# A graph network's gathers through a ring of eight lots instead of four

## The reference

```
h = relu(layernorm(x));  x = x + layer(h)          # four times

layer 0:  msg = relu(h[src] + edge_attr);           agg = segment_sum(msg, dst)
          out = ((1 + eps) * h + agg) @ W.T + b
layer 1:  relational attention: messages of 86 edge types from 16 bases,
          weighted by tanh(relu(score)), summed over dst, and a self loop
          that takes the source of each node's last edge
layer 2:  msg = edge_weight * h[src];               agg = segment_sum(msg, dst)
          out = relu(agg @ W + b)
layer 3:  msg = h[src];                             agg = segment_sum(msg, dst)
          out = agg @ W.T + b
```

## Time and profile before

| | us |
|---|---|
| median of 3 runs | 10165.41 |
| the profiled execution | 10155.89 |
| its span, first to last instruction | 10154.0 |
| POOL busy | 6668.1 (66%) |
| PE busy | 4395.6 (43%) |
| DVE busy | 4403.6 (43%) |
| ACT busy | 2227.0 (22%) |
| mean granted clock of TensorE | 0.538 |

### The profile page before, as it was taken

How to read it: one execution, slowest core, us unless ns; L and a number is a source line. 1 busy time by engine, 2 the same in 40 slices (tenths; PEclk the granted TensorE clock), 3 DMA queues, 4 the chain that set the end, 5 groups by cost and what they waited for, 6 DMA issues and landing times.

```text
span 10154.0 us, 102607 instructions
## 1 busy us (share of the span) xinstructions
PE 4395.6 (43%) x23835; PEld 3937.0 (39%) x23836; DVE 4403.6 (43%) x8860; ACT 2227.0 (22%) x5821; POOL 6668.1 (66%) x6577
## 2 busy tenths in 40 slices
PE   4444444444466666666663232222233232332223
PEld 3333333333366666666662222222222222222222
DVE  5444444444377777777773222222222222222222
ACT  0000000000477777777770000000000000000000
POOL 5666666664477777777775666666665666666665
PEclk6555555555655555555555555555555555555555
DMA  3111111111477777777771000000000000000001
GB/s 69 22 22 22 22 22 22 22 22 31 160 219 221 219 219 219 218 219 218 220 217 26 11 11 11 11 11 11 11 11 16 11 11 11 11 11 11 11 11 16
DMA packets 601171, 726.23 MB, mean 72 GB/s; under 512 B 341132, under 2 KB 434892, under 8 KB 597969
## 3 DMA queue, kind: packets, MB, share of 16 engines
q0 software_dynamic: 290064, 544.60, 21.8%
q1 hardware_dynamic: 311081, 181.32, 6.5%
HBM read 685.46 MB, written 40.38 MB: 71 GB/s over the span
## 4 chain that ended last, share of the span: by engine, by line
another core or an unknown queue 35%; issue 24%; POOL 22%; DVE 10%; DMA 3%; ACT 2%; PE 1%; DVEq 1%; POOLq 0%; SPq 0%; ACTq 0%
POOL arena L502 13%; POOL lanes L502 9%; DVE arena L978 3%; DMA lanes<-table,idx 2%; DVE arena L950 2%; DVE arena L942 1%; DVE lanes L942 1%; DVE lastrow L973 1%; ACT arena L699 1%; DMA arena<-table,idx 1%; DVE ps L937 0%; DVE lanes L968 0%; DVE lanes L1086 0%; ACT arena L685 0%
## 5 line engine op out<-in xcount | busy, mean ns | idle before, releaser
L502 POOL DMA_INDIRECT lanes<-table,idx x4764 | 4501.0, 945 | 2652.7 <-issue 1435.1
L1214 PE MATMUL ps<-arena,lanes 128*128 128x128 f32 x9528 | 2429.8, 425 | 4543.4 <-DVE arena L950 1844.0
L1214 PEld LDWEIGHTS ps<-arena,lanes 128*128 128x128 f32 x9528 | 2072.7, 303 | 4878.1 <-issue 4798.9
L502 POOL DMA_INDIRECT arena<-table,idx x1664 | 2049.1, 1231 | 676.9 <-issue 507.0
L551 ACT COPY idx<-tabs 128x4 int32 (+1 forms) x1616 | 303.0, 194 | 6851.8 <-DMA lanes<-table,idx 6698.3
L937 DVE TENSOR_TENSOR ps<-ps,tabs 128x16 f32<-128x16 f32 x1191 | 211.4, 177 | 3458.9 <-remote 3121.0
L1214 PE MATMUL ps<-lanes 128*128 128x32 f32 x3328 | 791.6, 402 | 666.0 <-issue 414.3
L1214 PEld LDWEIGHTS ps<-lanes 128*128 128x128 f32 x3328 | 750.3, 330 | 693.1 <-issue 693.0
L950 DVE TENSOR_TENSOR arena<-lanes,ps 128x512 f32<-128x512 f32 x794 | 543.7, 685 | 985.2 <-DMA lanes<-table,idx 944.6
L1311 PE MATMUL ps<-t,arena 128*128 x3328 | 955.5, 402 | 0.0
L1311 PEld LDWEIGHTS ps<-t,arena 128*128 128x128 f32 x3328 | 859.8, 318 | 0.0
(11 more groups left out here) (201 smaller groups left out, 3028.7 us busy)
## 6 DMA issues: line engine op xcount, KB each, us to landing
arena<-step_rows SPq DMA_DIRECT2D x416, 256.0 KB
lanes<-table,idx POOLq DMA_INDIRECT x4764
arena<-table,idx POOLq DMA_INDIRECT x1664
table<-arena SPq DMA_DIRECT2D x24, 1088.0 KB, 4.9
lanes<-in_edge_attr SPq DMA_DIRECT2D x388, 64.0 KB
table<-h SPq DMA_DIRECT2D x18, 256.0 KB, 2.4
edge_rows<-arena SPq DMA_DIRECT2D x1, 2496.0 KB, 8.4
lanes<-self_loop_table,selfi POOLq DMA_INDIRECT x98
```

Of the source, the lines that this page charges most:

```text
L502: pool.indirect_dma_start(out=to[:, k, u, :], out_offset=None, in_=tableD[l], in_offset=bass.IndirectOffsetOnAxis(ap=idx[:, k, u:u + 1], a ...
L1214: last = mm(ps[:, bass.ds(w[u], rhs.shape[-1])], onehot[:, k, u, :], rhs, start=False, stop=True, skip_group_check=True)
```

## The change

The ring of the wide layers becomes eight lots (`RING = 8`, `ROUND` = 32 tiles), so rows, attributes, indices, masks, both one-hot matrices and messages have eight slots. Only the sum with the attributes (`total`) keeps four. The narrow layer keeps its ring of four with arrays of its own (`idx1`, `onehot`, `msg`). In the wide layers each signal of an engine becomes one semaphore that counts lots through all three layers: `wide_idx_ready`, `total_ready`, `masked`, `weighted`, `wide_msg_ready` and `wide_mm_done`. A wait names the number of lots that must be done. What DMAs signal stays one semaphore for each slot, now eight. Layer 2 has 49 full rounds and five more lots, as have 0 and 3; no unused slots are counted up any more.

```diff
 LOTS, HB = 4, 4
 BODY = LOTS * HB
-STEPS_W = -(-(TILES + EXW) // BODY) * BODY
+RING = 8
+ROUND = RING * HB
+STEPS_W = -(-(TILES + EXW) // ROUND) * ROUND
+WIDE_LOTS = -(-(TILES + EXW) // HB)
+ROUNDS, REST = WIDE_LOTS // RING, WIDE_LOTS % RING
+BEFORE = {0: 0, 2: WIDE_LOTS, 3: 2 * WIDE_LOTS}
...
-        idx = sb("idx", [P, LOTS, HB], I32)
+        idx = sb("idx", [P, RING, HB], I32)
+        idx1 = sb("idx1", [P, LOTS, HB], I32)
...
-        masked = lotwise("mask_ready")
-        weighted = lotwise("weighted_mask_ready")
+        wide_idx_ready = sem("wide_idx_ready")
+        wide_gathered = [sem(f"wide_gathered_{h}") for h in range(RING)]
+        attr_loaded = [sem(f"attr_loaded_{h}") for h in range(RING)]
+        total_ready = sem("total_ready")
+        masked = sem("mask_ready")
+        weighted = sem("weighted_mask_ready")
+        wide_msg_ready = sem("wide_msg_ready")
+        wide_mm_done = sem("wide_scatter_done")
...
             with sp.Fori(0, MAIN) as i:
-                for k in range(LOTS):
-                    sp.wait_ge(row_used[k], i + 1)
+                for k in range(RING):
+                    sp.wait_ge(total_ready, i * RING + (k + 1))
...
+                def wide(i, lots):
+
+                    for k in range(lots):
+                        n = pool.to_reg(i * RING + (BEFORE[l] + k + 1))
+                        pool.wait_ge(written[0], written[1])
+                        pool.wait_ge(wide_idx_ready, n)
+
+                        pool.wait_ge(total_ready if l == 0 else wide_msg_ready, n)
+                        for u in range(HB):
+                            gather(grow[:, k, u, :], idx[:, k, u:u + 1], wide_gathered[k])
...
             def lots(l):
+
+                with act.Fori(0, ROUNDS - 1) as i:
+                    for k in range(RING):
+                        gathered_by(l, i, k)
+                        wide_lot(i + 1, k)
...
+                if l != 3:
+                    for k in range(RING):
+                        wide_lot(0, k)
...
+            def lots_to(l, i, k):
+
+                return i * RING + (BEFORE[l] + k + 1)
+
             def masks(l, i, k):
 
-                dve.wait_ge(mm_done[k], i + (BEFORE[l] + 1))
+                dve.wait_ge(wide_mm_done, lots_to(l, i, k))
                 tt(mask[:, k], iota_ps[:, 0:WB].unsqueeze(1).to_broadcast([P, HB, WB]), per_edge(BLK, i, k), ALU.is_equal
-                   ).then_inc(masked[k], 1)
+                   ).then_inc(masked, 1)
...
-                    tt(total[:, k], grow[:, k], attr[:, k], ALU.add).then_inc(row_used[k], 1)
-                    onehots(i, k, onehot)
+                    tt(total[:, k % LOTS], grow[:, k], attr[:, k], ALU.add).then_inc(total_ready, 1)
+                    onehots(i, k, onehotw)
...
+            def scatter(l, i, k, w):
+
+                pe.wait_ge(wide_msg_ready, i * RING + (BEFORE[l] + k + 1 + RING))
                 for u in range(HB):
...
-                last.then_inc(mm_done[k], 1)
+                last.then_inc(wide_mm_done, 1)
...
+                def body(i, lots):
+                    for k in range(lots):
+                        if k % LOTS == 0:
+                            w = windows(i * ROUND + k * HB, min(BODY, (lots - k) * HB))
+                        scatter(l, i, k, w[k % LOTS * HB:])
```

More of the change, by code:

```diff
@@ L52 @@
 XW = EXN + TILES
[L53 to L57, removed]
+NARROW = STEPS_N // BODY
+WIDE_LOTS = -(-(TILES + EXW) // HB)
+ROUNDS, REST = WIDE_LOTS // RING, WIDE_LOTS % RING
+BEFORE = {0: 0, 2: WIDE_LOTS, 3: 2 * WIDE_LOTS}
+TURN = {0: 0, 2: 1, 3: 2}
+MAIN = (N_EDGES // P) // ROUND
+TAIL = STEPS_W - MAIN * ROUND
+assert 0 < REST and MAIN + 1 == ROUNDS
 P1_LOTS = -(-BLOCKS // 4)
@@ L492, in _, with gather, narrow @@
                         pool.wait_ge(*written)
[L494 to L496 removed]
+                def gather(into, index, there):
+                    pool.indirect_dma_start(
+                        out=into, out_offset=None, in_=tableD[l],
+                        in_offset=bass.IndirectOffsetOnAxis(ap=index, axis=0)).then_inc(there, 16)
+                def narrow(n):
+                    for k in range(LOTS):
                         pool.wait_ge(written[0], written[1])
                         pool.wait_ge(idx_ready[k], n)
[L500 removed]
+                        pool.wait_ge(row_used[k], n)
                         for u in range(HB):
[L502 to L510, removed]
+                            gather(g1[:, k, u, :], idx1[:, k, u:u + 1], gathered1[k])
+                def wide(i, lots):
[6 more added lines that the diff above has]
+                            gather(grow[:, k, u, :], idx[:, k, u:u + 1], wide_gathered[k])
+                if l == 1:
+                    with pool.Fori(1, NARROW + 1) as n:
+                        narrow(n)
+                else:
+                    with pool.Fori(0, ROUNDS) as i:
+                        wide(i, RING)
+                    wide(ROUNDS, REST)
         @block.scalar
@@ L586, in linear @@
                 if l:
-                    for k in range(LOTS):
-                        act.wait_ge(mm_done[k], BEFORE[l + 1] + 1)
+                    act.wait_ge(wide_mm_done, BEFORE[l] + WIDE_LOTS + RING)
                     sums(0)
@@ L995, in scattered @@
             def scattered(l):
-                for k in range(LOTS):
-                    dve.wait_ge(mm_done[k], BEFORE[l + 1] + 1)
+                if l == 1:
+                    for k in range(LOTS):
+                        dve.wait_ge(mm_done[k], NARROW + 1)
+                else:
+                    dve.wait_ge(wide_mm_done, BEFORE[l] + WIDE_LOTS + RING)
             scattered(0)
```

186 lines of the change are left out of this document (96 added, 90 removed).

## The result

The changed kernel takes 10069.53 us (median of 4 runs, 10062.59 to 10080.74) and the kernel before 10168.27 (4 runs, 10157.7 to 10177.35): a ratio of 0.9904, 95% interval 0.9887 to 0.9921. It is 98.7 us faster. The forecast was 9850, so the direction is right, and the gain is less than a third of the 313 us forecast; the time lies outside the forecast's own range of 9760 to 10065, inside the wide one.

The account below looks back on a forecast made before the run. POOL's stops in layers 0, 2 and 3, from PE's signals held back while POOL gathers without pause. Savings 88 + 142 + 83 = 313 us off 10155.9, plus 9.5 for the median: 9850; own range 9760 to 10065, wide 9350 to 10160.

Parts of the forecast that it names:

- What bounds the kernel now: No engine is full; POOL's waits for DVE in layers 0, 2 and 3 total 1117.6 us, a deeper ring's most.
- PE is not late; its signal is: Layer 2: matmuls that DVE waits for had ended 37 and 24 us before DVE learned of it.
- the signals of x1 to x3 come in time for x5 to x7: Layer 2, lots numbered from DVE's release: signals of the first three scatters arrive in time for the lots four places on.
- 13 lots a cycle: Layer 2 with eight slots: POOL stops every 13 lots where it was 8, giving 30.5 stops.
- The stop was 8.05; I take 8.3: Layer 2: each POOL stop takes 8.3 us, 253 us in all, 142 less than 395.3.
- Layer 0: POOL stops every 8 lots for 6.0 us, the middle of two cases: 298 us in all, 88 less.
- Counters at nothing: Counting semaphores cost nothing; upper end 357 us, for a whole POOL pause of 0.30 us per lot.
- At a layer's end ... all at nothing, with some 5 us either way: ACT copies eight indices instead of four beside a layer's last scatters; this and other small changes cost nothing, 5 us either way.
- A: Signals are at most some 40 us late, so POOL never stops: 9047, or about 9600 with half the stops; chance 0.14.
- C: POOL issues four gathers between short pauses, such a lot costing 8.8 us instead of 5.9: 10520; chance 0.11.
- B: POOL's stops grow with its runs, so the ring buys nothing: 10165, between 10120 and 10185; chance 0.18.
- The rule of the Trainium skill: The block taking profile records holds up its producers rather than lose one inside; if so, records count, not the ring: 10165.

Follow-up runs that it names:

- the kernel with a gather in 1.55 us: Changed kernel with a POOL memset of 128x192 after each gather of the wide layers; 10450.38 us, 1.0423 of the kernel before.
- the short pause: Changed kernel with a POOL memset of 128x32 after each gather of the wide layers; 10089.44 us, 0.9898 of the kernel before.

## Why the prediction was wrong in size

**What bounds the kernel now.** Right in the main. POOL's stops are most of the loss: in a series without them the same kernel takes 8927 us instead of 10168, and layers 2 and 3 of the changed one 1982 and 1983 us, as worked out. Right too that layer 1 stays (2634). "PE is not late; its signal is" holds after the change as well, with signals 16 to 50 us late, and "one passing per some 20 us" is seen again (6814.14, 6835.20). What the rows of before could not show is that PE is slowed too, to one matmul in 2.1 to 2.9 us, when it is some 31 matmuls ahead of the last signal that got through.

**The step that failed: "the signals of x1 to x3 come in time for x5 to x7", and from it "13 lots a cycle".** With four slots PE takes up x1 at 6645.58, 1.8 us after DVE is released, and has scattered x1 to x3 by 1.4, 3.7 and 5.4 us after POOL's start. Their signals are through when DVE needs them, and a cycle is 4 + 3 + 1 = 8 lots. I kept the 3 for the ring of eight, added the four slots and one more signal, and got 13. But with eight slots PE has lots of the last cycle left when DVE is released at 6791.01, and takes up x1 only at 6796.71, 5.7 us later. DVE, with eight lots to catch up, asks for its signal at 6803.1, 12.1 us after the release and 9.7 after POOL's start. It is not there. The signal of x1, which had to be the first of three in time, comes at 6814.14, that of x2 at 6835.20, and POOL has run out of slots after 49.7 us: 8 + 0 + 2 = 10 lots. I had carried a number of signals over from one ring to the other where the trace only gave a time in which they pass. Nor is every cycle even that long: 25 of layer 2's runs are 40 gathers, others are shorter, and 397 lots with 51 waits for DVE are 7.8 lots each, where 13 were forecast (30.5 stops).

**"The stop was 8.05; I take 8.3".** The mean behind 40 gathers is 7.82, and 6.4 over all 51 waits of layer 2, so the size was fair or high. The count was wrong, and with it the idea that the stop is a fixed price that a longer run spreads: what stays is the stop time of a layer for each of its gathers. Predicted were 253 us in layer 2, 298 in layer 0 and 253 in layer 3; measured 328.1, 368.7 (230.5 for DVE's add and 138.2 "remote") and 317.4, against the 395.3, 386.2 and 336.1 of before. Part of this is in stops behind single lots, 12 of them in layer 2.

**Layer 0.** I took the middle between 9 lots and 7 for a run; the layer keeps its 5. The timeline of DVE there:

```profile
1322.50 0.18 DVE L987 TENSOR_TENSOR ps<-ps,tabs 128x16 f32<-128x16 f32 x1 [9.18 <-remote]
...
1332.31 0.17 DVE L987 TENSOR_TENSOR ps<-ps,tabs 128x16 f32<-128x16 f32 x1
...
1340.24 0.30 DVE L1025 TENSOR_TENSOR lastrow<-ps,last 128x16 bf16<-128x16 f32 x2 [5.12 <-remote]
...
1352.31 0.18 DVE L987 TENSOR_TENSOR ps<-ps,tabs 128x16 f32<-128x16 f32 x1 [9.10 <-remote]
```

Four lots at 2.45 us, the fifth begun at 1332.31, 8.6 us into POOL's run and held back until 1343.2, and no sixth before POOL stops at 1348.37. The sixth, at 1352.31, had waited for a lot whose matmuls ended at 1329.49, 22.8 us before. I had seen the slow fifth lot and still used it for the lower end only. The stops behind runs of 20 gathers are 4.03 us instead of 4.97 in the mean, but others were added; of the 31 us that the layer gained, 18 are in the waits for DVE.

**Counters at nothing.** 28 us with the ring kept at four (interval 16 to 41). Without the hold-up counters and ring together cost nothing (0.9984); the counters were not run alone there. The range of 0 to 357 held it, and zero was a little low.

**"At a layer's end ... all at nothing, with some 5 us either way".** Some 20 us between layers 0 and 1, from a ring that is left full.

**The rivals.** A (the hold-up is bounded) would have been 9047 and is out: with twice the ring the stops remain. C (dribbling) is out as a price, though single lots between pauses are there. B, "the stop grows with the run", had 0.18 and is the nearest to what the runs show, though its "fewer pieces" did not come; it put the time at 10165 and is 95 us off, less than half of the forecast's error of 220. It was held unlikely for parts of the stop that "do not grow". What the runs don't explain is why a gather of layer 2 comes to 1.46 us with the ring of eight and to 1.49 with four (2318 and 2364 us over 1588); such 2% are the whole gain of the change.

**The rule of the Trainium skill** ("NOTIFIC — the notification-queue block", section "7.1 Overflow: three behaviours, one of which stalls the engine") led to B's time, and the traces bear on it. Without the hold-up the trace of the changed kernel holds 131294 semaphore updates, with it 34869; for one slot's `wide_gathered`, which each gather raises by 16, it has 9600 of 9600 and 1352. All 104067 instructions are in both. The updates of gathers are by far the most numerous. In the wide layers records and stops go together: the kernel with a gather in 1.55 us, run in the series with the hold-up, has no stops and 25903 of 27759 updates in layer 2, the changed kernel 4312 of 27359. In layer 1 they don't: there about half or more are missing in every trace with the hold-up (17362 of 38597 after), and the layer is only 39 us longer. This agrees with a limit on records more than with any other cause tried. Against it stands that eight signals more of DVE for each lot cost so little. The same section has records held up inside rather than lost, and here records are missing. No kernel was run without recording, nor a gather with fewer than its 16 updates; that the hold-up is the recording's is argued, not shown.

## What to carry to other kernels

Before a stall is spread over a deeper buffer, ask whether it is a price per stop or a rate: divide each stop by the work done before it, in two layers if there are two. If the quotient is the same (here 4.97/20 and 8.06/32), expect a ring to change where the pieces lie more than their sum, and look for fewer of the operations that cost the rate: a kernel that leaves out a quarter of the gathers took 16% less, a ring of twice the depth 1%. An experiment that puts the idle time in on purpose (the short pause) shows such a rate in one run. And when a number of signals "come in time", write down until when, and ask whether the engine that sends them will be as early in the new kernel.

## What the runs showed of the hardware that was not expected

- One program took 10168, 10189, 10182 and 10022 us in four series and 8922 and 8927 in two, 14% apart, one of each kind under the same chip number. Where the hold-up is missing, the change is worth 0.16% instead of 1%.
- With the hold-up and a gather each 1.25 us, PE's signals reached DVE 16 to 50 us after the matmuls in the cycle shown, against 0.01 us without it. With four slots PE kept its full pace in layers 2 and 3 all the same. With eight it fell to a matmul in 2.1 to 2.9 us, from some 9 us after POOL's start until 6 us after its stop, being 31 matmuls ahead of the last signal that got through in 92 of 113 waits. DVE was slowed too: layer 0's fifth lot took 10.9 us (1332.31 to 1343.2) instead of 2.45. At one gather in 1.55 us nothing of this is left in the wide layers.
- Rows and bytes of a gather have no part in it: 64 rows instead of 128, in the same number of packets, left the wide layers at 2348, 2323 and 2300 us.
- TensorE's granted clock in layer 2 is higher in the series with the hold-up (a mean of 0.57, and 0.59 with three gathers a lot) than in those without (0.50, the 1.2 GHz level throughout): PE's matmuls come in bursts after long gaps in the one and evenly in the other. A higher mean clock is here no sign that PE gets on better.
